# Values' bias by a one-row product, operand loads in half as many transfers, the first head's loads and the angles moved into the projection

## The reference

```python
q = split_heads(x @ Wq + bq)      # 16 heads of 8
k = split_heads(x @ Wk + bk)
v = split_heads(x @ Wv + bv)
scores = einsum('bhqd,bhkd->bhqk', q, k) / sqrt(8)
av = einsum('bhqk,bhkd->bhqd', softmax(scores), v)
x = layernorm(x + av @ Wo + bo)
```

## Time and profile before

| what | us |
|---|---|
| median of 3 runs | 1731.61 (1728.04 to 1735.49) |
| the profiled execution | 1729.86 |
| its span, first to last instruction | 1728.1 |
| busy: TensorE, VectorE, ScalarE, GpSimd | 1574.9, 1393.2, 1187.2, 787.9 |
| mean granted clock of TensorE | 0.961 of full |

### The profile page before, as it was taken

How to read it: one execution, slowest core, us unless ns; L and a number is a source line. 1 busy time by engine, 2 the same in 40 slices (tenths; PEclk the granted TensorE clock), 3 DMA queues, 4 the chain that set the end, 5 groups by cost and what they waited for, 6 DMA issues and landing times. The chain is left out here.

```text
span 1728.1 us, 41224 instructions
## 1 busy us (share of the span) xinstructions
PE 1574.9 (91%) x14986; PEld 806.7 (47%) x14986; DVE 1393.2 (81%) x2949; ACT 1187.2 (69%) x2461; POOL 787.9 (46%) x605
## 2 busy tenths in 40 slices
PE   6499999999999999968999998999999989699887
PEld 4122223223223232244777775667777755344454
DVE  6799999999999999646999996689999968343355
ACT  5168888888888888865788784267888744555421
POOL 4211111112221114247888882288888825644301
PEclk9589999999999999988999999999999999999999
DMA  5203111000000000111223222322232222000001
GB/s 166 75 20 129 34 36 38 20 20 20 21 20 20 21 22 17 49 51 39 59 57 83 61 54 62 80 53 62 57 92 62 55 57 66 1 1 2 1 18 32
DMA packets 124384, 79.14 MB, mean 46 GB/s; under 512 B 50594, under 2 KB 110940, under 8 KB 123932
## 3 DMA queue, kind: packets, MB, share of 16 engines
q1 hardware_dynamic: 122796, 75.44, 16.4%
q10 hardware_dynamic: 1392, 1.12, 0.2%
HBM read 42.82 MB, written 16.79 MB: 34 GB/s over the span
## 5 line engine op out<-in xcount | busy, mean ns | idle before, releaser
L1101 DVE TENSOR_REDUCE hd_top<-hd_pX 128x1 f32<-128x512 f32 x1024 | 623.6, 680 | 32.8 <-PE hd_pX L935 32.8
L1069 ACT ACTIVATE hd_E<-hd_pS 128x1024 f32<-128x1024 f32 x512 | 524.7, 1025 | 82.1 <-PE hd_pS L951 59.9
L935 PE MATMUL hd_pX<-l_K,l_Q 48*128 48x512 bf16 x1024 | 342.3, 396 | 26.1 <-DMA l_Q<-q_parts 21.5
L968 PE MATMUL hd_pO<-hd_E,l_V 128*32 128x256 f32 x4096 | 327.6, 392 | 18.0 <-ACT hd_O L1044 18.0
L951 PE MATMUL hd_pS<-l_Q,l_K 50*128 50x512 bf16 x1024 | 310.5, 384 | 3.0 <-DMA l_Q<-hd_negp 2.0
L883 POOL TENSOR_TENSOR hd_inv<-hd_OS,hd_minus 128x16 f32<-128x16 f32 x31 | 90.0, 2902 | 443.4 <-ACT hd_OS L1057 430.8
L1815 POOL TENSOR_TENSOR w_inv<-w_ss,w_mhalf 128x16 f32<-128x16 f32 x64 | 186.4, 2913 | 0.0
L1710 ACT ACTIVATE w_pS<-w_pS,w_nb 128x128 f32<-128x128 f32 x512 | 178.5, 365 | 6.5 <-DVE w_nb L1901 4.7
L1804 POOL TENSOR_TENSOR w_C<-w_C,w_N 128x1024 f32<-128x1024 f32 x64 | 151.0, 2360 | 61.3 <-DVE w_N L1875 61.0
L968 PEld LDWEIGHTS hd_pO<-hd_E,l_V 128*32 128x32 f32 x4096 | 81.7, 108 | 171.3 <-issue 124.7
L951 PEld LDWEIGHTS hd_pS<-l_Q,l_K 50*128 50x128 bf16 x1024 | 59.0, 94 | 197.8 <-issue 184.7
(11 more groups left out here) (290 smaller groups left out, 2785.0 us busy)
## 6 DMA issues: line engine op xcount, KB each, us to landing
w_VA<-w_V SPq DMA_DIRECT2D x127, 128.0 KB, 2.3
l_Q<-q_parts SPq DMA_DIRECT2D x192, 32.0 KB
l_K<-k_parts SPq DMA_DIRECT2D x168, 32.0 KB
m<-early_rows SPq DMA_DIRECT2D x64, 64.0 KB, 1.7
f_H<-m SPq DMA_DIRECT2D x32, 128.0 KB, 2.7
f_X<-m SPq DMA_DIRECT2D x16, 256.0 KB, 3.0
q_parts<-pj_ptq SPq DMA_DIRECT2D x8, 384.0 KB, 2.5
k_parts<-pj_ptk SPq DMA_DIRECT2D x8, 384.0 KB, 2.5
```

Of the source, the lines that this page charges most:

```text
L935: nc.tensor.matmul(px[:, :], Q[m.j][rows, m.z, b, t * P:(t + 1) * P], K[m.j][rows, b, k * 512:(k + 1) * 512], start=True, stop=True).then_ ...
L968: last = nc.tensor.matmul(pO[VW * b:VW * b + VW, cols], V[n.j][:, b * NT + g, :], E[g % SLOTS][:, b, cols], start=(g == 0 and half == 0), ...
L1069: nc.scalar.activation(E[g % SLOTS][:, 2 * k:2 * k + 2, :], pS[k][:, :, :], ACT.Exp).then_inc(exped[k], 1)
L1101: nc.vector.tensor_reduce(top2[m.z][:, ROW_ORDER[q], k:k + 1], pX[slot][:, :], AX.X, ALU.max).then_inc(topped, 1)
```

## The change

- **Values' bias.** TensorE first multiplies a row of ones by the row of the bias into the values' PSUM bank (one row deep, 512 columns), and the four products of the values add to it. VectorE's addition goes; ScalarE copies the values out instead, behind the queries and keys of the same chunk.
- **Loads.** A new class `HeadLoads` loads a head's operands in runs of 3, 2 and 1 bands, for queries and for keys and for both groups: 6 transfers and 6, where there were 12 and 12. The source of the queries has the parts as its leading index; that of the keys repeats one part by a leading index of step zero.
- **Where head 0 is loaded.** SyncE issues its queries at the end of the projection, behind the wait for all stores, and ScalarE its keys, behind a wait for the keys' stores. Both wait for the first buffer's memsets.
- **Angles.** VectorE computes them at the very start of the projection, before its loop. In the heads phase ScalarE issues the keys of head 1 before it takes the sines.
- Every memset of the operand buffers now increments a semaphore.

```diff
+class HeadLoads:
+    RUNS = [(0, 3), (3, 2), (5, 1)]
+    COUNT = 16 * 2 * GROUPS * len(RUNS)
+
+    def queries(self, eng, h, j):
+        for band, n in self.RUNS:
+            of_head = self.q_parts[0:n, bass.ds(h * HD, HD), :].rearrange("a r (z g c) -> a r z g c", z=2, g=GROUPS)
+            for r in range(GROUPS):
+                first = GROUP_ROWS * r + band * HD
+                rows = self.Q[j][first:first + n * HD].rearrange("r z b t -> r z (b t)")
+                eng.dma_start(rows, of_head[:, :, :, r, :]).then_inc(self.loaded[j], 16)
+
+    def keys(self, eng, h, j):
+        for part, (band, n) in enumerate(self.RUNS):
+            of_head = self.k_parts[part:part + 1, bass.ds(h * HD, HD), :].rearrange("a r (g c) -> a r g c", g=GROUPS)
+            for r in range(GROUPS):
+                first = GROUP_ROWS * r + band * HD
+                rows = self.K[j][first:first + n * HD].rearrange("r b t -> r (b t)")
+                eng.dma_start(rows, of_head[:, :, r, :].broadcast_to([n, HD, GB * S])).then_inc(self.loaded[j], 16)
...
 @block.sync
+                sp.wait_ge(cleared, 3)
+                loads.queries(sp, 0, 0)
                 sp.wait_ge(zeroed, 16 * len(zero_rows))
 @block.tensor
+                pe.wait_ge(ones_set, 1)
...
+                        nc.tensor.matmul(pM["v"][j][:, :].rearrange("p (t d) -> p t d", t=CT), ones[:, :],
+                                         bvr[:, :].rearrange("p (t d) -> p t d", t=1).broadcast_to([1, CT, D]),
+                                         start=True, stop=False, skip_group_check=True)
                         for t in range(CT):
                             last = nc.tensor.matmul(pM["v"][j][:, t * P:(t + 1) * P], XT[:, j, t * P:(t + 1) * P], w["v"][:, :],
-                                                    start=True, stop=True)
+                                                    start=False, stop=True, skip_group_check=True)
 @block.scalar
+                        act.wait_ge(made["v"][j], i + 1)
+                        out = v_all[:, bass.ds((2 * i + j) * CT, CT), :]
+                        nc.scalar.copy(out, pM["v"][j][:, :].rearrange("p (t d) -> p t d", t=CT)).then_inc(taken["v"][j], 1)
+                for j in range(2):
+                    act.wait_ge(stored["k"][j], 16 * (T // CH // 2))
+                act.wait_ge(cleared, 3)
+                loads.keys(act, 0, 0)
 @block.vector
-                dve.wait_ge(weights_in, 16 * 7)
+                kept.angles(dve)
...
-                        dve.wait_ge(made["v"][j], i + 1)
-                        out = v_all[:, bass.ds((2 * i + j) * CT, CT), :]
-                        nc.vector.tensor_tensor(out, pM["v"][j][:, :].rearrange("p (t d) -> p t d", t=CT),
-                                                bvr[:, :].rearrange("p (t d) -> p t d", t=1).broadcast_to([P, CT, D]), ALU.add)\
-                            .then_inc(taken["v"][j], 1)
 @block.gpsimd
+                nc.gpsimd.memset(ones[:, :], 1.0).then_inc(ones_set, 1)
...
 phase_l0_heads, @block.scalar
-                load(act, 0, 0, K, k_parts, 1)
                 kept.load_ident(act, a)
+                loads.keys(act, 1, 1)
                 kept.sines(act)
-                load(act, 1, 1, K, k_parts, 1)
 phase_l0_heads, @block.vector
-                kept.angles(dve)
```

More of the change, by code:

```diff
@@ L429, in phase_l0_project @@
         bqs = s.sb("bqs", [P, 1])
-        bvr = s.sb("bvr", [P, D])
+        bvr, ones = s.sb("bvr", [1, D]), s.sb("ones", [1, P])
         X = s.sb("X", [P, 2, CT, D])
@@ L441, in phase_l0_project @@
         bias_scaled = s.sem("bias_scaled")
-        cleared = s.sem("cleared")
+        cleared, ones_set = s.sem("cleared"), s.sem("ones_set")
         x_in = s.sems("x_in")
@@ L554, in _ @@
                 Q, K, V = operands
+                nc.gpsimd.memset(ones[:, :], 1.0).then_inc(ones_set, 1)
                 for j in range(len(K)):
-                    nc.gpsimd.memset(K[j][:, :, :], 1.0)
-                    nc.gpsimd.memset(Q[j][:, :, :, :], 0.0)
+                    nc.gpsimd.memset(K[j][:, :, :], 1.0).then_inc(cleared, 1)
+                    nc.gpsimd.memset(Q[j][:, :, :, :], 0.0).then_inc(cleared, 1)
                     nc.gpsimd.memset(V[j][:, :, :], 0.0).then_inc(cleared, 1)
-                pool.wait_ge(cleared, len(K))
+                pool.wait_ge(cleared, 3 * len(K))
                 for j in range(len(K)):
@@ L696, in vector, with phase_l0_heads @@
         self.shift(dve, len(self.ORDER) - 1)
-def phase_l0_heads(nc, s, kept, a, q_parts, k_parts, v_all, attn, operands, x_out_d, landing, following):
+def phase_l0_heads(nc, s, kept, a, q_parts, k_parts, v_all, attn, operands, x_out_d, landing, following, loads):
     UNITS = 2 * H
@@ L733, in phase_l0_heads @@
         pO = s.ps("pO", [P, HQ])
-        loaded = s.sems("loaded", R)
+        loaded = loads.loaded
         v_ready = s.sems("v_ready", R)
@@ L755, in phase_l0_heads @@
         tail = ProjectTail(nc, s, kept, attn, a["L0_attn_embedding"], x_out_d, landing, following, pX, pS)
-        LOADS = 16 * 2 * GROUPS * len(PART_PAIRS)
+        LOADS = loads.COUNT
         NEGS = 16 * MAX_ROWS * GROUPS
@@ L800, in phase_l0_heads @@
         with nc.Block() as block:
-            def load(eng, h, j, dst, src, part):
-                for band, parts in enumerate(PART_PAIRS):
-                    for r in range(GROUPS):
-                        first = GROUP_ROWS * r + band * HD
-                        rows = dst[j][first:first + HD]
-                        of_head = src[parts[part], bass.ds(h * HD, HD), :]
-                        if part == 0:
-                            rows = rows.rearrange("r z b t -> r z (b t)")
-                            of_head = of_head.rearrange("r (z g c) -> r z g c", z=2, g=GROUPS)[:, :, r, :]
-                        else:
-                            rows = rows.rearrange("r b t -> r (b t)")
-                            of_head = of_head.rearrange("r (g c) -> r g c", g=GROUPS)[:, r, :]
-                        eng.dma_start(rows, of_head).then_inc(loaded[j], 16)
             @block.sync
@@ L829, in load_both @@
                 def load_both(h, j):
-                    load(sp, h, j, Q, q_parts, 0)
-                    load(sp, h, j, K, k_parts, 1)
+                    loads.queries(sp, h, j)
+                    loads.keys(sp, h, j)
                 def head(h, j):
@@ L843, in head @@
                         kept.load(sp, a, h)
-                for h in range(2):
-                    load(sp, h, h, Q, q_parts, 0)
+                loads.queries(sp, 1, 1)
                 store_neg(0, 0, 0)
@@ L2766, in build @@
                         [s0.sb(f"V{j}", [P, TILES, VW]) for j in range(buffers)])
+            loads = HeadLoads(heads, operands, q_parts, k_parts)
             phase_l0_project(nc, kept, a, a["L0_attn_embedding"], a["L0_attn_Wq"], a["L0_attn_bq"], a["L0_attn_Wk"], a["L0_attn_bk"],
                              a["L0_attn_Wv"], a["L0_attn_bv"], a["ident"], q_parts, k_parts, v_all, list(pad.values()), a["zeros"],
-                             operands)
+                             operands, loads)
             landed = Landing(shores, "xa_stored", T // CH // 2)
             start = LocalStart(nc, layers, kept, pad["xa"])
-            phase_l0_heads(nc, heads, kept, a, q_parts, k_parts, v_all, attn, operands, tokens["xa"], landed, start)
+            phase_l0_heads(nc, heads, kept, a, q_parts, k_parts, v_all, attn, operands, tokens["xa"], landed, start, loads)
         with ExitStack() as rooms:
```

8 lines of the change are left out of this document (6 added, 2 removed).

## The result

The changed kernel took 1742.09 us (median of 6 runs, 1739.0 to 1746.06), the kernel before 1730.19 beside it (6 runs). The ratio is 1.0067, 95% interval [1.0042, 1.0092]: 11.6 us longer (the two medians differ by 11.9), a little beyond the 0.5% that tells from no change. The profiled execution took 1740.33, its span is 1738.5, and the mean clock is 0.963.

A forecast was written before the change was run, and what follows sets the result against it. The change was taken to be worth its effect on the heads' first product, at 63.62 us: +4.7 us at the last split and +2.5 for head 0's loads on 1729.86 gave 1737.1, stated as 1737.5; range 1727 to 1745.

The forecast's parts named there:

- The angle chain, 20.0 us: VectorE at the projection's start: angles, held up by GpSimd's memsets, end at 20.0 us, where the first split starts.
- a waiting step gets one gap between memsets: Angle chain on VectorE: each held step gets in when the current memset ends, paying up to 1.8 us.
- The upper bound of 22: Latest end of the angle chain, in us, if a gap or two between memsets is missed.
- held-up against unhindered angles: Projection's last split: 53.8 us if memsets hold the angles up, 48.2 if nothing does.
- Values' bias: Projection: VectorE's two-chunk turn takes 7.7 us instead of 9.1, TensorE's 7.9 at full clock, each one-row product 0.86.
- The turns: Projection: X of turn 2 reaches TensorE 4.26 us behind the split; last split at 53.8 instead of 49.13, +4.7 us.
- Rival (d): Projection: TensorE keeps the low clock through turns 2 and 3; sum +18 us, 1747; chance 0.06.
- The loads of head 0, 17.0 us behind the last split: Before the heads: merged transfers run on 3, 2 and 8 DMA engines, delaying the first product by +2.5 us.
- The slow end of this term: Head 0's loads: with packets at 18 GB/s an engine, the first product comes +5 us later.
- -1.4 for twelve issues at the new place: Head 0's loads: if each transfer is issued part by part, first product 13.1 us behind the last split, -1.4.
- Later heads' loads hidden: Heads: SyncE already waits about 10 us each for ScalarE's turned maxima, so fewer issues win nothing and slower transfers cost nothing.
- The waits for `cleared`, keys of head 1 ahead of the sines: Waits met by GpSimd's first memsets; keys take 6 x 0.5 us on ScalarE ahead of the sines; both cost nothing.

The follow-up runs named there:

- angles_only: The kernel before with only the angle chain moved to the start of the projection; ratio 1.0043 to the kernel before.
- after_ones_v: The changed kernel with the row of ones set by VectorE instead of GpSimd; ratio 1.0055 to the kernel before.
- best2: Changed kernel with 12 and 12 loads, ones set by VectorE, angles ending VectorE's projection part, sines ahead of head 1's keys; ratio 0.9997 to the kernel before.
- ones_only: The kernel before with only a short GpSimd memset of a 1x128 tile, which nothing reads, ahead of its memsets; ratio 1.0027 to the kernel before.
- bias_only: The kernel before with the values' bias part alone, the ones set by GpSimd; ratio 1.0006 to the kernel before.
- old_loads: The changed kernel with 12 and 12 operand transfers for every head, at the new places; ratio 1.0044 to the kernel before.
- bias_ones_v: The kernel before with the values' bias part alone, the row of ones set by VectorE; ratio 1.0018 to the kernel before.
- signals_v: The changed kernel with only the memset of the values' operand signalling, head 0's loads waiting for one signal; ratio 1.0076 to the kernel before.

## Why the prediction came out as it did

The time, 1742.09, lies in the range and 4.6 us above the forecast of 1737.5; in the whole it is slower by 0.67%, for which the prediction had a chance of 0.28, and not within 0.5%. In kind it was right: angles held up by memsets, few DMA engines, heads unchanged. Two terms were too small by together 10.1 us, and 5.7 us that it did not know of came back. That the time lies in the range is luck to this extent: without those 5.7 us it would have been 1747.8, beyond the upper end of 1745.

- **The angle chain, 20.0 us.** Measured 23.24. Which steps wait was right: the six one-element steps ran free (0.15 to 0.16 us each), the 128x4 step waited. That "a waiting step gets one gap between memsets" is the step that failed: here it got none. It held in angles_only and in after_ones_v, where the first split starts at 19.73 and 19.75. The short memset of the ones, which the prediction had costed at nothing ("met by GpSimd's first memsets"), made the difference, by itself or by the 0.14 us by which it moves the others: 4.7 us at the last split, 5.8 at the first product. The upper bound of 22 ("a gap or two missed") was too low; the bound that the rows gave was the end of the long memsets, 18.9, plus the rest of the chain, 4.6.
- **The angles' move itself.** after_ones_v and best2 have the same projection except for it: 54.16 against 47.35, so 6.8 us; angles_only against before gives 7.0. The prediction's own steps give 53.8 - 48.2 = 5.6 for held-up against unhindered angles.
- **Values' bias.** Forecast: VectorE's turn 7.7, TensorE's 7.9 at the full clock. Measured: splits of turn 0 from 23.24 to 30.86, 7.62. The one-row product takes 1.05 us from its start to the next (50.48 to 51.53), not 0.86. A turn of TensorE at the clock 1.00 takes 9.4 us (turn 3, 47.14 to 56.55), not 7.9. In best2, where nothing else is in the way, the last split ends at 47.35 against 49.13: the part is worth 1.8 us there, but this holds a gain of clock too, since from 12 us to the last split the mean is 1.00 in best2 and 0.84 in before. Between ones_only and bias_only, both with a held CAST, it is 1.4. In bias_only the long CAST turns this into a loss of 2.7.
- **The turns.** X of turn 2 reached TensorE 4.79 us behind the split (30.86 to 35.65), forecast 4.26. TensorE's turn 2 lasted 11.5 us (35.65 to 47.14), forecast 10.1; with the 3.2 of the angles this makes the 5.0 by which 58.82 exceeds 53.8. The low clock lasted 5.5 us of turn 2, where the prediction's row had it for 4.5. Rival (d), a low clock through turns 2 and 3, did not happen, though its sign, a low clock for more than half of turn 2, was missed only narrowly (5.5 of 11.5 us): turn 3 lasts 9.4 us from its transposes (47.14) to its last values, where the prediction had 16 for the low clock.
- **The loads of head 0, 17.0 us behind the last split.** Measured 22.07. The division was right, and 0.18 of 16 engines with head 0 alone shows it. That rule of the Trainium skill (DMA: Bandwidth & Descriptors, section "Why a DMA increments its semaphore by 16 and not by 1") is borne out: 2.9 engines busy where it gives three and, for a small part, eight. What failed is that head 1 was left out of the sum. Its keys stood in the working as 3 us of ScalarE ahead of the sines, and its queries not at all; neither was counted as packets on the same three engines. They were issued from 68.40 and 67.99 us on, while head 0's were still moving, and together they cost 3.7 us. The Trainium skill (DMA: Bandwidth & Descriptors, section "Queues, rings and completion order") has an engine take turns between the queues that have work for it, a packet at a time; the 3.7 us agree with it in kind, and the prediction hadn't weighed it. The remaining 1.3 is the rate: 17.7 had been worked out at 22 GB/s an engine, and 17.0 was chosen for fewer engines at a better rate. The engines gave 21. The slow end of this term was summed too low as well: at 18 GB/s the prediction's own terms give +5.9, not +5, and +7.6 was measured. Its -1.4 for twelve issues at the new place, on the other hand, is what old_loads shows.
- **Later heads' loads hidden.** Right: SyncE's wait for the turned maxima in 31 waits is now 392.2 us in total, where the earlier trace rows has 319.9; the shorter issues only lengthened it, and the heads kept their length.
- **The waits for `cleared`, keys of head 1 ahead of the sines.** The waits for `cleared` were met long before (the third memset ends at 5.31 us). The keys cost nothing on ScalarE: the sines ended at 74.7, ahead of the first product.
- **Small slips of the sums.** The hand-over of turn 3 adds up to 46.4, not 46.1. The times beside the rivals leave out the 1.75 us that the forecast of 1737.5 adds for the median. Neither changes a reading.

In one sum: bias -1.8, angles +6.8, gaps closed +4.7, together 9.7 at the last split; earlier place -1.4, three engines +5.3, head 1 on them +3.7, together 7.6; 17.3 at the first product, and 11.6 in the whole. The terms are differences of single profiles in a chain, so they must add up, and each is less sure than it looks. With the other kernels that have the same part, gaps closed is 2.9 to 4.7, the earlier place 1.1 to 2.6, the merged transfers (three engines and head 1 together) 7.6 to 9.0, and head 1 among them 2.6 to 3.7.

## What to carry to other kernels

Work moved into another engine's idle time must be looked at with what runs beside it there: the angles were free under a wait for loads and cost 6.8 us under memsets, while VectorE had a truly empty stretch behind its last split. When transfers are merged, count the engines that the merged form runs on, and then everything else that will be on those same engines, the next tile's loads first. And before a gain or loss of a few microseconds is read off one profile, look whether the granted clock differs in stages that the edit doesn't touch.

## What the runs showed of the hardware

- A VectorE step can be held through many of GpSimd's memsets, and for the first step that waits it was one or the other here: in 5 profiles of 14 it got in at the next end of a memset or, in before and best2, at the one after (longest waits 0.95 to 1.75 us), in 9 it was held until the last long one was over (10.6 to 10.8 us for the 128x4 step, 5.6 to 6.2 for the CAST). A memset of 0.19 us stood ahead of the others in 8 of the 9 and in none of the 5; adding it (ones_only) closed the gaps, and moving it to VectorE opened them in after_ones_v but not in bias_ones_v. The Trainium skill (SBUF — State Buffer, section "SBUF: two separate sides") says that the two engines contend for a pair of ports as "an **exclusive lock**, not a bandwidth split", held for a whole instruction, which fits a wait for one memset. By itself it would let VectorE in when that memset ends, and nine of the traces here show otherwise. In them the next memset starts about 0.05 us before the recorded end of the last, and the first break, 0.06 us in the changed kernel (18.45 to 18.51), is behind the last long one; but the profiles in which VectorE got in have the same overlap, so that alone doesn't explain it.
- Where VectorE gets in, GpSimd's next memset is longer: 2.09 us instead of 1.81 beside a CAST of 128x512, 1.83 beside a step of 128x32.
- Transfers of two queues on the same three DMA engines slow each other: holding head 1's back shortened head 0's by 3.7 us (2.6 against the nearest other kernel), at 21 GB/s an engine.
- The instant at which TensorE's clock rises differs between profiles of the same projection: at 38.3 us in signals_v and at 41.2 in the changed kernel, with the last split at 57.07 and 58.82.
